# Writing out the loop over the middle head groups in a Mamba-2 block with a SwiGLU feed-forward

## The reference

```python
x = x + mamba(layernorm(x))        # 128 heads of 64, 8 groups of 16 heads, state 128
x = x + ffn(layernorm(x))          # SwiGLU of width 1376, each of its 3 products with a LoRA part

def mamba(u):
    gate, xBC, dt = split(u @ in_proj_w.T)          # 8192, 8192 + 2*8*128, 128 columns
    xBC = silu(conv1d(xBC, 4 taps) + conv_b)
    hs, Bm, Cm = split(xBC)
    y = ssd(hs, -exp(A_log), Bm, Cm, D, softplus(dt + dt_bias))   # scan over the tokens
    g = y * silu(gate)
    g = g * rsqrt(mean(g*g over each group) + eps) * norm_w
    return g @ out_w.T
```

## Time and profile before

| | us |
|---|---|
| median of three runs (lowest, highest) | 1957.95 (1957.22, 1965.29) |
| the profiled execution's own time | 1957.61 |
| its span, first to last instruction | 1955.8 |
| PE busy in the span | 1827.1 (93%) |
| DVE, ACT, POOL busy | 1200.4, 1143.8, 1065.2 |
| start of group 0, group 1, group 7 on PE | 115.5, 313.6, 1534.0 |
| start of the last chunk on PE | 1706.3 |

### The profile page before, as it was taken

The page is one execution under the profiler, slowest core; times in us unless marked ns, Lnnn a source line. Parts: engine busy times, 40 slices in busy tenths (PEclk is TensorE's granted clock), DMA queues, the critical chain, the costliest instruction groups (busy, mean ns, idle before and its releaser), DMA issues.

```text
span 1955.8 us, 31241 instructions
## 1 busy us (share of the span) xinstructions
PE 1827.1 (93%) x9826; PEld 1455.9 (74%) x9826; DVE 1200.4 (61%) x2070; ACT 1143.8 (58%) x2185; POOL 1065.2 (54%) x989
## 2 busy tenths in 40 slices
PE   5879999999899999999999989998999997679999
PEld 4668787878777877787778778786878786457767
DVE  6467677767676668675867676667666775622112
ACT  4666667666766666666666666666666764322111
POOL 3346666666666656665656565655666664431121
PEclk9989999999999999999999999999999999889989
DMA  3523334434433443434433353334333432221101
GB/s 119 159 84 115 104 116 144 119 101 119 142 117 101 119 138 95 121 97 116 128 101 119 113 146 105 115 103 124 103 115 105 147 105 70 83 66 42 30 21 44
DMA packets 118769, 205.94 MB, mean 105 GB/s; under 512 B 23888, under 2 KB 28368, under 8 KB 118576
## 3 DMA queue, kind: packets, MB, share of 16 engines
q1 hardware_dynamic: 118576, 203.62, 34.4%
HBM read 198.85 MB, written 4.72 MB: 104 GB/s over the span
## 4 chain that ended last, share of the span: by engine, by line
PE 76%; DVE 11%; issue 5%; POOL 4%; ACT 3%; DMA 1%; SPq 0%; DVEq 0%; POOLq 0%; ACTq 0%
PE bank L1280 14%; PE bank L1282 13%; PE bank L1281 13%; PE bank L1343 7%; PE bank L1381 4%; PE bank L1383 4%; PE bank L1382 4%; PE bank L1356 4%; PE bank L1369 3%; PE bank L1321 3%; DVE x_ch L1068 2%; DVE ow_l L1074 2%; DVE xdt L1087 1%; DVE bcT L1068 1%; PE bank L1534 1%
## 5 line engine op out<-in xcount | busy, mean ns | idle before, releaser
L596 POOL TENSOR_TENSOR w_l<-w_raw,w_h 128x512 fp32r<-128x512 f32 x288 | 372.6, 1297 | 321.3 <-ACT w_h L726 320.1
L1280 PE MATMUL bank<-x_h,w_h 128*128 128x512 f32 x1160 | 474.6, 409 | 24.2 <-DVE x_ch L1068 11.0
L1282 PE MATMUL bank<-x_h,w_l 128*128 128x512 f32 x1160 | 460.4, 397 | 0.0
L1281 PE MATMUL bank<-x_l,w_h 128*128 128x512 f32 x1160 | 460.1, 397 | 0.0
L1068 DVE SCALAR_TENSOR_TENSOR x_ch<-bank,par,x_ch 128x511 f32<-128x511 f32 (+2 forms) x384 | 287.4, 749 | 128.4 <-ACT x_ch L743 119.4
L774 ACT ACTIVATE decay<-decay,cols 128x128 f32<-128x128 f32 x1024 | 317.0, 390 | 0.7
L1280 PEld LDWEIGHTS bank<-x_h,w_h 128*128 128x128 f32 x1160 | 220.3, 190 | 89.5 <-issue 25.6
L602 POOL TENSOR_SCALAR_AFFINE_SELECT decay<-decay 128x512 f32<-128x512 f32 x256 | 199.5, 792 | 126.9 <-DMA decay<-cum_scratch 126.9
L1282 PEld LDWEIGHTS bank<-x_h,w_l 128*128 128x128 f32 x1160 | 219.8, 190 | 52.2
L1281 PEld LDWEIGHTS bank<-x_l,w_h 128*128 128x128 f32 x1160 | 220.6, 190 | 45.8
L1381 PE MATMUL bank<-ow_h,gT_h 128*128 128x512 f32 x512 | 226.4, 442 | 16.2 <-POOL gT_l L620 16.2
(11 more groups left out here) (135 smaller groups left out, 2845.7 us busy)
## 6 DMA issues: line engine op xcount, KB each, us to landing
w_raw<-in_wp SPq DMA_DIRECT2D x288, 256.0 KB, 3.4
decay<-cum_scratch SPq DMA_DIRECT2D x256, 256.0 KB, 3.7
ec<-ecum_scratch SPq DMA_DIRECT2D x96, 256.0 KB, 4.8
ow_raw<-in_ow SPq DMA_DIRECT2D x64, 256.0 KB, 4.6
raw<-in_w SPq DMA_DIRECT2D x20, 256.0 KB, 2.9
w_raw<-in_w SPq DMA_DIRECT2D x10, 256.0 KB, 3.7
acc<-in_x SPq DMA_DIRECT2D x8, 256.0 KB, 5.3
out<-acc SPq DMA_DIRECT2D x8, 256.0 KB, 2.0
```

The source lines that it names most:

```text
L596: pool.tensor_tensor(w_l[:, s, :], w_raw[:, s, :], w_h[:, s, :].bitcast(F32), ALU.subtract).then_inc(wl_ready, 1)
L1280: pe.matmul(dst, wh, xh, start=(k == 0), stop=False)
L1281: pe.matmul(dst, wh, xl, start=False, stop=False)
L1282: last = pe.matmul(dst, wl, xh, start=False, stop=(k == len(terms) - 1 and not more))
```

## The change

The loop of the sequencer becomes a Python loop in all five lists, so that `body` is emitted six times, with `g` a Python number. Nothing else differs: the same operations in the same order, with the same waits, now against constants; no register work, no branch.

```diff
@@ SP (L541)
             body(0, False)
-            with sp.Fori(1, GROUPS - 1) as g:
+            for g in range(1, GROUPS - 1):
                 body(g, False)
             body(GROUPS - 1, True)
@@ POOL (L686)
-            with pool.Fori(1, GROUPS - 1) as g:
+            for g in range(1, GROUPS - 1):
@@ ACT (L912)
-            with act.Fori(1, GROUPS - 1) as g:
+            for g in range(1, GROUPS - 1):
@@ DVE (L1225)
-            with dve.Fori(1, GROUPS - 1) as g:
+            for g in range(1, GROUPS - 1):
@@ PE (L1472)
-            with pe.Fori(1, GROUPS - 1) as g:
+            for g in range(1, GROUPS - 1):
```

## The result

The written-out kernel takes 1925.68 us (median of 4 runs, 1924.43 to 1926.69); the kernel before, measured beside it, 1960.56 us (4 runs, 1957.22 to 1965.29). The ratio is 0.9823, with a 95% interval from 0.9800 to 0.9847: 1.8% faster, or 34.9 us between the medians. The forecast was 1923.9 us, a range of 1917 to 1934 us, and 34.0 us of gain.

The account below looks back on a forecast made before the run. PE was taken as the bound, idling at taken loop branches and then running at a lower clock. Savings of 20.1 + 11.1 + 2.9 = 34.1 us (34.0 by group windows) gave 1923.9 us from the 1957.95 us median, range 1917 to 1934 us.

Parts of the forecast that it names:

- The taken branches of PE: Chunk 7 of groups 1 to 5: PE stands still at its taken loop branch; removing the branches was to save 20.1 us.
- The clock behind them: Chunk 0 of groups 2 to 6: lower PE clock after each taken branch; running at full clock was to save 11.1 us.
- The register work: Groups 1 to 6: register instructions for waits that depend on `g` fall away, 0.49 us a group, 2.9 us (0 to 6).
- The other four lists: DVE, ACT, POOL and SP also lose branches and register work; costed at nothing beyond the other terms.
- Longer code: Five more copies of the body to fetch, in packets of 16 KB; cost taken as 0, at most 1 us each.
- rival C: Every 16 KB of PE's list: code fetches not hidden, 56 packets at 1 us, 22 us slower, 1980 us; chance 0.04.
- Rivals A and B: A: clock still falls at seams, 1935 us, chance 0.06; B: another wait replaces the branch, 1955 to 1958 us, chance 0.03.
- Head and feed-forward: Parts outside the loop keep their code; could shift by 2 or 3 us, depending on where the lower clock falls.
- The sign of being right that failed: In the changed kernel's trace, all eight group windows but the last were to take 197.5 to 198.5 us.

## Why the prediction was right

**The taken branches of PE, 20.1 us.** Right: chunk 7 of groups 1 to 5 fell from 113.36 to 5 x 18.52 = 92.6 us, 20.8 us. That it is this branch and no other wait is shown by the loop on PE alone, which brings back the whole time. That it is the fetch of the target is shown by the hint, which takes the branch down to 0.35 us and makes the exit stop instead, and by the packet that falls into the stop.

**The clock behind them, 11.1 us.** Right: chunk 0 of groups 2 to 6 fell from 152.54 to 140.54 us, 12.0 us, with a clock of 1.00 in each. That the pause brings the clock down is shown by the empty loops: behind 2.68 us it fell at all five seams, behind 0.87 us at none.

**The register work, 2.9 us.** Right: of the 34.3 us by which the six groups got shorter, 20.1 and 11.1 us are the two terms above, which were worked out against chunks in loop form, and 3.1 us are left. The windows show where they lie. Chunk 3 (here of group 1, before and after) falls by 0.19 us in each group, chunk 7 without a taken branch from 18.66 to 18.52 us, and chunk 0 without a stop from 28.28 to 28.04 us; the other chunks are the same in both forms.

```profile
394.89:413.60 18.71, 17.77 (x106) 14.30 (x105) 9.55 (x19) 13.67 (x29) 11.70 (x11) 1.00 0.37 109
396.49:415.01 18.52, 17.73 (x107) 14.31 (x106) 9.56 (x19) 13.42 (x28) 11.71 (x11) 1.00 0.35 109
```

Some luck is in the 2.9 us: the group 0 that it took for written out ends at the entry into the loop, and its chunk 7 (18.62 us) is itself 0.1 us longer than that of straight code. PE's own share is small: with PE alone in a loop, chunk 3 takes 18.54 us, against 18.52 us written out and 18.71 us with the other four lists in loops; DVE's loop alone makes 18.62 us.

**The other four lists at nothing.** Right for this change, where all five loops go at once, and it was said why. But the text took it from the waits of those engines that none of them would hold PE, and that holds only under PE's cover: uncovered, they cost 13.1 us. The rows had it: DVE waited for PE's L1343 until 517.68, but its sequencer had not been free before 515.7, and written out it starts L1118 1.7 us after L1343. A wait that ends on PE doesn't show how early the engine would have been ready.

**Longer code at nothing.** Right, rival C is out: six straight groups within 0.2 us of one another, with 9 of PE's packets in the second of them. Rivals A and B are out too; the clock is 1.00 and nothing took the place of the stop.

**Head and feed-forward.** The shift of 2 or 3 us that the range allowed for came, at 2.8 us of the span and all of it a loss. Group 7, whose code is the same in all these kernels, took 172.3 us before, 173.15 us after, and up to 175.5 us in the experiments without a hint. The rows above put the losses in group 0 and group 7 where the clock is lower than before. Why it is lower there was not tested; that the low stretches fall on other work because the groups start at other times was only argued. The sign of being right that failed is here: group 0 lasts 198.66 us, over the 197.5 to 198.5 us named for all but the last group.

The rule of the Trainium skill that was weighed, 108 ns for a compare-and-branch ("Advanced Engine Details and Errata", section "Control Flow Timing"), is near the branch that isn't taken (83 ns) and within a factor of two of short branches back (208 ns). It would have predicted a gain of 3 us; the gain is that of the branches taken to code that is not at hand. The Trainium skill's page "Runtime: NRT & Kernel Launch", section "Instruction fetch mechanics", says that a taken branch whose target is not among the blocks at hand waits for it. The runs agree: 3.8 us of stop with a packet in it, and 0.59 us with the hint.

## What to carry to other kernels

A branch back over a long body costs its engine the fetch of code (3.6 to 5.5 us on PE here, against 0.2 us in an empty loop), and where PE is the bound, the clock adds some 2 us more. Write such a loop out in every list: with PE's alone written out 20 of 34 us came, with the other four alone 0, and with one other list left in a loop 6 to 12 us were missing. In the trace, look for idle time with releaser "issue", then for the sequencer's own row of the loop line, and compare the pass that falls through with the others.

## What the runs showed that was not expected

- A prefetch hint moves the stop and doesn't remove it: 0.59 and 1.08 us at the entry of each pass instead of 3.81 us, and then 3.2 to 3.5 us at the exit, where there was none.
- A pause of 2.68 us costs nearly as much in clock (9.7 us over five seams) as one of 8.57 us (11.1 us); one of 0.87 us costs nothing beyond itself.
- A short branch back on PE takes 208 ns, but a pass of an empty loop with it 0.36 us (8.57 us for 24).
- Stops of DVE, SP and ACT at the same seam are not additive: 11.8, 13.6 and 7.7 us alone, 13.1 us for all of them with POOL. ACT's sequencer was away for 5.7 us alone and 2.5 us beside the others.
